# A gated cross-attention and expert layer on one core: another order of the opening, inputs laid out by the host, and the first block's routing moved

## The reference, cut to what matters

```python
x = x + tanh(g_xattn) * (softmax(q k^T / 4) v  W_o^T + b_o)   # q from layernorm(x), k and v from the context, 16 heads of 16
z = layernorm(x); h = layernorm(z) * ln_g + ln_b              # second half
logits = h @ Wr; top 2 of 7 experts, softmax of the two values as gates
# each expert takes at most 732 tokens, counted in the order of first choices, then second choices
routed = sum over kept choices of gate * (silu(h @ W1) * (h @ W3)) @ W2
shared = (silu(h @ W1s) * (h @ W3s)) @ W2s
x = x + tanh(g_ffn) * (routed + shared)
```

## Time and profile before

| | us |
|---|---|
| median of 3 runs | 910.91 (910.74 to 912.74) |
| the profiled execution, its own time | 909.93 |
| its span, first to last instruction | 908.2 |
| PE busy | 826.7 (91%) |
| DVE busy | 609.4 (67%) |
| ACT busy | 385.8 (42%) |
| POOL busy | 326.0 (36%) |

### The profile page before, as it was taken

How to read it: one execution, slowest core, us unless ns; L and a number is a source line. 1 busy time by engine, 2 the same in 40 slices (tenths; PEclk the granted TensorE clock), 3 DMA queues, 4 the chain that set the end, 5 groups by cost and what they waited for, 6 DMA issues and landing times.

```text
span 908.2 us, 14547 instructions
## 1 busy us (share of the span) xinstructions
PE 826.7 (91%) x5130; PEld 713.9 (79%) x5130; DVE 609.4 (67%) x1360; ACT 385.8 (42%) x718; POOL 326.0 (36%) x259
## 2 busy tenths in 40 slices
PE   4766799998999999999899999999999999999991
PEld 3533686885866858758687789999999999999991
DVE  5566877878779778787777766566665656565340
ACT  3254235336344254263535345354444545453330
POOL 5171403104013031040112840846547281823333
PEclk9868799999999999999999999999999999999996
DMA  6542041122400423203113332334434333431111
GB/s 170 139 140 63 10 117 36 44 74 49 117 15 21 116 49 69 56 27 93 36 43 119 110 99 93 83 87 103 85 102 82 86 74 104 97 66 19 16 19 19
DMA packets 97297, 66.93 MB, mean 74 GB/s; under 512 B 57910, under 2 KB 84716, under 8 KB 97240
## 3 DMA queue, kind: packets, MB, share of 16 engines
q1 hardware_dynamic: 43624, 55.40, 21.8%
q0 software_dynamic: 53088, 10.30, 8.3%
q10 hardware_dynamic: 528, 0.52, 0.2%
HBM read 37.38 MB, written 14.27 MB: 57 GB/s over the span
## 4 chain that ended last, share of the span: by engine, by line
PE 68%; DVE 13%; issue 7%; POOL 2%; ACT 1%; DVEq 0%; DMA 0%; POOLq 0%
PE bank L1367 19%; PE bank L1369 18%; PE bank L1368 18%; PE bank L1583 2%; PE bank L1584 2%; PE bank L1585 2%; DVE hidden L1097 2%; PE bank L1448 1%; PE bank L1621 1%; DVE bn_parts L1049 1%; DVE normed_heads L1101 1%; DVE row_max L1087 1%; DVE float_data L1170 1%; PE bank L1549 1%; DVE float_data L1068 1%
## 5 line engine op out<-in xcount | busy, mean ns | idle before, releaser
L1367 PE MATMUL bank<-split_operands 128*128 128x366 f32 (+4 forms) x1148 | 385.7, 336 | 15.2 <-DVE split_operands L1017 9.7
L1368 PE MATMUL bank<-split_operands 128*128 128x366 f32 (+4 forms) x1148 | 379.4, 331 | 0.0
L1369 PE MATMUL bank<-split_operands 128*128 128x366 f32 (+4 forms) x1148 | 379.3, 330 | 0.0
L1367 PEld LDWEIGHTS bank<-split_operands 128*128 128x128 f32 (+1 forms) x1148 | 217.2, 189 | 36.9 <-DVE split_operands L1022 7.2
L1369 PEld LDWEIGHTS bank<-split_operands 128*128 128x128 f32 (+1 forms) x1148 | 216.5, 189 | 12.4
L1368 PEld LDWEIGHTS bank<-split_operands 128*128 128x128 f32 (+1 forms) x1148 | 217.5, 189 | 9.7
L836 POOL DMA_INDIRECT out<-float_data,scatter_now x42 | 125.5, 2987 | 179.6 <-issue 93.0
L1350 DVE TENSOR_TENSOR hidden<-bank,float_data 128x366 f32<-128x366 f32 x112 | 60.4, 540 | 113.9 <-PE bank L1369 113.9
L1003 ACT ACTIVATE float_data<-bank 128x366 f32<-128x366 f32 x112 | 53.5, 477 | 113.7 <-PE bank L1369 113.7
L1000 ACT CAST split_operands<-hidden 128x366 fp32r<-128x366 f32 x112 | 55.7, 497 | 68.4 <-DVE hidden L1350 67.3
L812 POOL DMA_INDIRECT float_data<-z_scratch,gather_now x42 | 72.1, 1718 | 14.9 <-issue 14.0
(11 more groups left out here) (152 smaller groups left out, 1099.9 us busy)
## 6 DMA issues: line engine op xcount, KB each, us to landing
float_data<-in_L_ffn_W SPq DMA_DIRECT2D x21, 1024.0 KB, 8.6
split_operands<-split_operands SPq DMA_DIRECT2D x96, 128.0 KB, 2.3
float_data<-in_x SPq DMA_DIRECT2D x8, 512.0 KB, 4.8
z_scratch<-float_data SPq DMA_DIRECT2D x8, 512.0 KB, 3.1
out<-float_data SPq DMA_DIRECT2D x7, 512.0 KB, 2.8
split_operands<-split_operands SPq DMA_DIRECT2D x8, 192.0 KB, 3.8
float_data<-in_L_ffn_W1s SPq DMA_DIRECT2D x2, 512.0 KB, 4.1
float_data<-in_L_ffn_W3s SPq DMA_DIRECT2D x2, 512.0 KB, 4.9
```

The lines of the kernel that those rows point to most:

```text
L1367: pe.matmul(o, lhs[0], rhs[0], start=first, stop=False)
L1368: pe.matmul(o, lhs[0], rhs[1], start=False, stop=False)
L1369: return pe.matmul(o, lhs[1], rhs[0], start=False, stop=last)
```

## The change

1. **Inputs.** The host lays out the context (`ctx`), the four attention weights (`att`, with the rows of W_o already permuted) and all small inputs (`small`: biases, gains, gates, router) by partition. SP's first DMAs are twelve in place of 35 (three shared halves among them in both): the 16 loads of W_o and most of the small ones are gone.
2. **Opening.** The old steps are cut finer (`norm` into `stats_x`, `scale_x`, `residual`; queries and projection into the product and its reading out) and put in another order, below. W_v and W_o's low parts go from DVE to POOL. The four maxima of block 0 come before `project_values`; norm, transposes and queries of block 1 come after them, the queries between the halves of block 0's scores.
3. **Keys.** `kbd` is filled as soon as the high keys are there (`first_keys`), before the keys' scratch is written.
4. **Shared weights.** Halves 0 to 2 are loaded and cast beside block 0's maxima, 3 to 5 after block 0's projection; the low parts are made on POOL in three groups (6, 2 and 4 pieces), the second of them ahead of `norm2(0)`'s inverse root on POOL's queue.
5. **`norm2(0)`** stands between the third and the fourth maxima of block 1. With it, SP's store of z and load of x come before `stack_maxima(1)`.
6. **Block 0's routing.** `transpose_z(0)`, `logits(0)`, `logits_T(0)`, `choose(0)`, `count(0)`, `counted(0)`, `slots(0)` and `place(0)` and the norm of block 2 move from the end of `first_period` and the start of period 1 into the later part of period 1.
7. **Banks.** Block 0 and 1 use two PSUM banks (4, 5) in turn for the value products, with a new semaphore `pv_read` for when DVE has read one; the other banks are dealt out anew.

```diff
 def first_period(do, b):
     n = b.next()
+    do("context")
+    do("weights", 1)
     do("project_keys")
-    do("norm", b)
-    do("keys_lo")
+    do("stats_x", b)
+    do("weights", 0)
+    do("scale_x", b)
+    do("bias_keys")
     do("transpose_x", b)
-    do("norm", n)
+    do("weights", 2)
     do("queries", b)
+    do("queries_out", b)
+    do("keys", b)
+    do("residual", b)
+    do("stack", b)
+    do("shared_weights", 0)
+    for t in range(TT):
+        do("maxima", b, t)
     do("project_values")
-    do("keys", b)
-    do("stack", b)
-    do("maxima", b, 0)
-    do("maxima", b, 1)
-    do("transpose_x", n)
-    do("maxima", b, 2)
-    do("maxima", b, 3)
     do("maxima_T", b)
     do("stack_maxima", b)
+    do("values_out")
+    norm(do, n)
+    do("first_scores", b)
+    do("transpose_x", n)
     do("route_const")
+    do("scores", b, 0)
     do("queries", n)
-    do("first_scores", b)
-    for half in range(2):
-        do("scores", b, half)
+    do("scores", b, 1)
+    do("queries_out", n)
     do("stack", n)
+    do("attention_hi", b)
     do("maxima", n, 0)
     do("maxima", n, 1)
-    do("attention_hi", b)
     do("project", b)
+    do("project_out", b)
+    do("shared_weights", 1)
     do("maxima", n, 2)
+    do("norm2", b)
     do("maxima", n, 3)
     do("maxima_T", n)
     do("stack_maxima", n)
-    do("norm2", b)
-    do("transpose_z", b)
+    do("shared_rest")
     do("first_scores", n)
-    do("logits", b)
-    do("logits_T", b)
-    do("choose", b)
-    do("norm", n.next())
...
     do("scores", b, 0)
     if b.at(1):
-        do("count", f)
-        do("counted", f)
-        do("slots", f)
+        do("transpose_z", f)
     do("scores", b, 1)
+    if b.at(1):
+        nxt("stats_x")
     up(0)
-    do("place", f)
+    if b.at(1):
+        nxt("scale_x")
+        nxt("residual")
+    else:
+        do("place", f)
     do("attention_hi", b)
+    if b.at(1):
+        do("logits", f)
     up(1)
+    if b.at(1):
+        do("logits_T", f)
     nxt("transpose_x")
     up(2)
     do("project", b)
+    do("project_out", b)
     nxt("queries")
+    nxt("queries_out")
     nxt("stack")
     do("norm2", b)
+    if b.at(1):
+        do("choose", f)
     down(0)
     down(1)
     nxt("maxima", 0)
     up(3)
-    do("transpose_z", b)
-    up(4)
+    if b.at(1):
+        do("count", f)
+        do("counted", f)
+        do("slots", f)
+        up(4)
+        do("place", f)
+        do("transpose_z", b)
+    else:
+        do("transpose_z", b)
+        up(4)
     down(2)
     do("logits", b)
...
+def pv_bank(b, p):
+    return 4 + (p // 2 % 2 if b.at(0) or b.at(1) else p // 2)
...
         def transpose_x(b):
...
+            if b.at(2):
+                pe.wait_ge(sig["lg_done"], 1)
...
         def maxima(b, t):
             if b.at(0):
                 if t == 0:
-                    pe.wait_ge(sig["v_ready"], B)
...
         def logits(b):
...
+            if b.at(1):
+                pe.wait_ge(sig["place_added"], 1)
...
         def count(b):
             pe.wait_ge(sig["r_onehots"], b.n + 1)
+            if b.at(0):
+                pe.wait_ge(sig["m_done"], 2 * TT + 1)
...
-            if p == 4:
-                if b.at(1):
-                    pe.wait_ge(sig["hl_ready"], KD)
...
-            if p == 6 and b.at(1):
-                pe.wait_ge(sig["counts_read"], 1)
+            if b.at(0) or b.at(1):
+                if p >= 4:
+                    pe.wait_ge(sig["pv_read"], b.n * 4 + p // 2 - 1)
```

More of the change, by code:

```diff
@@ L189, in period @@
     if not b.at(NB - 2):
-        do("norm", n.next())
+        norm(do, n.next())
     down(7)
@@ L542, in _ @@
         sp.sem_inc(out_stored[1], 16)
[L543 to L555, removed]
@@ new lines, in load_shared, with first_keys @@
+        def load_shared(h):
+            if h >= 3:
+                sp.wait_ge(sig["wsplit_lo"], NSTEP0 + 2 * (h - 2))
+            if h == 5:
+                sp.wait_ge(sig["xT_ready"], 2 * KD)
+            m, part = h // 2, h % 2
+            kk = wsv[m].shape[1] // 2
+            sp.dma_start(sh_stage[h].rearrange("p (k f) -> p k f", k=kk), wsv[m][:, part * kk:(part + 1) * kk])\
+              .then_inc(shared_loaded[h % 3], 16)
+        for h in range(3):
+            load_shared(h)
+        def first_keys():
+            sp.wait_ge(sig["zeros_ready"], 1)
+            sp.wait_ge(sig["k_hi"], KD)
+            for j in range(8):
+                sp.dma_start(kbd[16 * j:16 * j + 16, :, j, :].bitcast(F32), k_s[16 * j:16 * j + 16, 0, :, 0:SK].bitcast(F32))\
+                  .then_inc(sig["kbd_loaded"], 16)
@@ L586, in project_keys, with more_shared @@
                 sp.dma_start(kscr[j].rearrange("(k p) t -> p k t", p=P), k_s[:, j].bitcast(F32)).then_inc(sig["k_stored"], 16)
[L588 to L595, removed]
-        for h in range(3):
-            load_shared(h)
-        def load_more_shared(b, half):
-            if b.at(0) and half == 0:
+        def more_shared(half):
+            if half == 1:
                 for h in range(3, 6):
@@ L608, in load_keys @@
                 bt = b.i
[L609 to L615, removed]
+                if not b.at(0):
+                    sp.wait_ge(sig["m_done"], b.n * TT)
+                    kd = kscr.rearrange("s (g j d) (b t) -> s j d g b t", g=KD, j=8, b=B)
+                    for j in range(8):
+                        sp.dma_start(kbd[16 * j:16 * j + 16, :, j, :].bitcast(F32), kd[0, j, :, :, bt, :])\
+                          .then_inc(sig["kbd_loaded"], 16)
                 sp.wait_ge(sig["k_stored"], 32)
@@ L819, in first_gather @@
             gather(Turn(0, 1))
-        token_blocks(pool, {"norm": norm, "scores": attention_lo, "stack": stationary_values, "norm2": norm2,
+        token_blocks(pool, {"stats_x": stats_x, "residual": residual, "weights": weights, "shared_weights": shared_weights,
+                            "shared_rest": shared_rest, "values_out": first_values, "scores": attention_lo, "stack": stationary_values, "norm2": norm2,
                             "route_const": route_const, "first_pieces": split_pieces, "slots": onehot_values,
@@ L1299, in last_pieces @@
                                   W1_[:, 0, m, cols].bitcast(F32), ALU.subtract).then_inc(sig["wsplit_lo"], 1)
-        token_blocks(dve, {"project_keys": project_keys, "keys_lo": keys_lo, "project_values": project_values, "norm": norm, "scores": scores, "transpose_x": transpose_x, "project": project,
-                           "queries": queries, "norm2": norm2, "transpose_z": transpose_z, "logits_T": logits_T,
+        token_blocks(dve, {"context": context, "weights": weights, "bias_keys": bias_keys, "values_out": values_out,
+                           "stats_x": stats_x, "scale_x": scale_x, "scores": scores, "transpose_x": transpose_x,
+                           "project_out": project_out, "queries_out": queries_out, "norm2": norm2, "transpose_z": transpose_z, "logits_T": logits_T,
                            "maxima": maxima, "up": up, "last_hidden": last_hidden, "shared_out": shared_out,
```

326 lines of the change are left out of this document (181 added, 145 removed).

## The result

The kernel after takes 926.18 us (median of 4 runs, 923.78 to 926.47), beside 911.60 us for the kernel before on the same chip. The ratio is 1.0155, with a 95% interval of 1.0142 to 1.0167: slower by some 14.6 us. The profiled execution took 926.31 us at a span of 924.1 us, 15.9 more than the span before. The prediction had the direction, but its 914.7 us and its range, 906 to 920, are too low.

The account below looks back on a forecast made before the run. The prediction took PE, busy 91% of the span, as the bound. Its terms, 6.5 - 1.9 - 9.4 = -4.8 us, made the profiled 909.93 us into 914.7, with a range of 906 to 920.

Parts of the forecast that it names:

- the large give-back: Period 1, first down to block 1's logits: 9.4 us lost, as block 0's routing delays place(0).
- Step 1: Opening, up to block 1's first scores: at 75.7 instead of 77.95 us, 2.2 us earlier.
- Scaling 1.4: norm2(0)'s scaling on VectorE, ahead of block 1's fourth reduction, was taken to last 1.4 us.
- the 0.8 us for SP's two transfers: Delay of block 1's stacked maxima by z's store and x's load just ahead: 0.8 us, between bounds 0 and 5.6.
- Step 2: Block 1's scores up to up(0,0): at 91.0 instead of 97.56 us, 6.5 us earlier.
- Rival 3: Clock falls in period 1, at the gap ahead of place(0) and once more, 2 us each: 918 us; chance 0.14.
- Step 3: Period 1, first down to block 1's logits: 20.7 us instead of 11.3, so 9.4 us given back.

Follow-up runs that it names:

- e1: The kernel after, with GpSimd's last four low parts of the shared weights made to wait until norm2(0)'s scaling is done: 922.46 us, ratio 1.0113.
- e10: e1 with GpSimd's pieces 6 and 7 also moved behind norm2(0)'s inverse root: 920.00 us, ratio 1.0086.
- e3: The kernel after, with 58 extra unused matmuls in TensorE's gap, around the transposes of block 1's maxima: 922.00 us, ratio 1.0115.
- e8: e2 with choose(0) right behind logits_T(0), and count, counted and slots ahead of the first down: 915.95 us, ratio 1.0028.
- e2: The kernel after, with only norm2(0) moved back behind stack_maxima(1): 919.12 us, ratio 1.0057.
- e4: e2 with block 0's routing and block 2's norm put back where the kernel before has them: 911.66 us, ratio 0.9985.
- e6: e4 with e1's wait and 28 extra unused matmuls in TensorE's gap ahead of block 1's scores: 907.22 us, ratio 0.9946.
- e9: e8 with the 58 extra matmuls of e3: 918.31 us, ratio 1.0063.

## Why the prediction was wrong in size

**What held.** All of the difference is made ahead of block 1's logits, and the large give-back is the one that was named. From the first `down` to `place(0)` the prediction had 15.3 us and the trace has 15.45; the idle time there was to be some 4 us and is 4.23, released by GpSimd's one-hot values; ahead of `count` 1.2 and 1.40. From `up(0,0)` to the first `down` 1.9 us were to be given back, and 1.4 were. Block 0's first scores came 1.7 us earlier than predicted. Some sums of the walk are 0.1 to 0.4 us above their own terms (GpSimd free at 34.8, where 23.8 + 2.8 + 7.8 is 34.4); none of this makes the miss.

**Step 1 that failed: "To block 1's first scores: only 2.2 us earlier".** They came 3.8 later, a miss of 6.0 us. Two terms of the step were wrong. "Scaling 1.4" ran beside GpSimd's pieces and took 5.16, which is 3.8 of the miss (e1: 3.5 us at this mark, 3.7 in time). And the load that was to be issued at 60.1, with GpSimd's two pieces done at 66.6, was issued at 62.40, and they ended at 69.6: 3 us more (e10 gives 2.0 at the mark, since VectorE's third reduction ends only at 69.2 there). Against this stands the 0.8 us for SP's two transfers, which do not show: from the issue of the stacked maxima at 79.37 it is 2.35 us to the first score, as before.

The load was late in the main because block 0's scores were long. Timelines: VectorE's low parts of block 1's queries after, then the load's issue in e3.

```profile
56.42 1.37 DVE L1147 SCALAR_TENSOR_TENSOR split_operands<-bank,small_inputs,split_operands 128x512 fp32r<-128x512 f32 x2
...
59.57 0.59 SPq L621 DMA_DIRECT2D float_data<-in_L_ffn_W3s  x1
```

From block 0's first scores to these low parts the walk has 21.0 us (35.1 to 56.1), and the trace 24.4 (33.41 to 57.79), with the clock at 0.50 in the midst of it. In e3, where the clock rose early, the load is issued at 59.57.

I carried over 1.4 us from a row with a free GpSimd without bounding it. The trace of before could have warned me. Timeline of DVE before: one kind of operation beside GpSimd's pieces of 45.91 to 61.46, and with GpSimd idle.

```profile
47.27 1.44 DVE L1101 TENSOR_TENSOR normed_heads<-hidden,recip_den 128x256 f32<-128x256 f32 x1
...
163.92 0.42 DVE L1101 TENSOR_TENSOR normed_heads<-hidden,recip_den 128x256 f32<-128x256 f32 x1
```

For a scaling there was no such row, but there was one for its engine. The Trainium skill, SBUF — State Buffer, "SBUF: two separate sides", says that VectorE and GpSimd share a pair of SBUF ports, and that the pair is an exclusive lock, held for a whole instruction, between a GpSimd operation and a VectorE operation in a two-port mode or with two SBUF inputs. An estimate by this section of the Trainium skill, if the scalings run in such a mode and each waits for one piece of 1.27 us, is 4 x 1.27 = 5.1 us. The trace agrees with 5.16; the mode and the port it does not show.

**Step 2: "To up(0,0): 6.5 us earlier".** The walk had 15.3 us from the first scores; it was 19.4. It priced exponentials and waits at the rows' durations and took no fall of the clock in this stage. The wait of 5.12 us is gone as predicted, but with the clock at 0.50 TensorE is busy for 17.16 us of the stage, and it is as long as before. e3 shows the size: 14.4 us at 0.92. Rival 3 had this kind of cost, but priced it in period 1 and at 2 us a time; of the opening it said only that it has such gaps.

**Step 3, mis-sized: "Downs to logits(1): 9.4 us given back".** It was 11.0. The order and the waits are as predicted up to `place(0)`. Behind it the clock was low: `place` took 1.88 us (0.97 in e8) and the transposes of z 1.93 (1.03 in the earlier trace rows), and the `down` behind them began at the low clock too. This is rival 3 in the place that it named, worth 1.6 us.

The sum: 6.0 for step 1, 4.1 for step 2, 1.6 for step 3, less 0.5 for the stretch to the downs, is 11.2. Added to the predicted 4.8 it is 16.0, and the spans differ by 15.9.

**The move of `norm2(0)`** by itself costs 7.1 us (e2), and e2 is still 0.6% slower than the kernel before. The rest is the routing's place: e4 brings 7.5 us of it back.

## What to carry to other kernels

A step on a second engine's queue has to be read twice: for what waits behind it, and for what runs beside it. Before costing a VectorE operation from SBUF at its usual duration, look at what GpSimd does in those microseconds; a single wait on GpSimd was worth 3.7 us here. And where a chain of small steps stands decides what it costs: block 0's routing made block 1's scores 1.4 us longer (20.8 in e4, 19.4 in e2), and the stretch to block 1's logits, where TensorE has no time to spare, 12 us longer (41.7 against 29.6). Last, read an experiment's trace ahead of the stage that it is about: the profiled executions of e3 and e9 were some 3 us ahead before their first extra matmul ran.

## What the runs showed of the hardware that I had not expected

- Four VectorE `tensor_scalar` of 128x256 from SBUF to SBUF took 5.16 us beside GpSimd's 128x512 `tensor_tensor` (5.17 in e2) and 1.38 alone. VectorE's reduction of 128x462 from PSUM beside the same GpSimd operation, at 67.14, took 1.54 us for three of them, its usual time.
- After 4.66 us without TensorE work (e2), and after waits of 1.83 and 0.76 us with little work between them (e6), the granted clock was 0.50 for the next 24 and 16 us, though TensorE was busy for most of that time. In the kernel before it was back at 1.00 by 84 us, 6 us into block 1's scores, though TensorE was busy for only 13.15 of their 19.61 us. Why it rises in the one and not in the other is open.
- In block 0's scores the clock rose to 1.00 by 42 us in two traces (e3, e9) and only near 49 us in the other traces of the new opening. Block 1's last maxima came some 3 us sooner with it.
- A store and a load of 512 KB each, issued some 3 us ahead of two small copies within SBUF, did not delay them: 2.35 us from issue to use, as without them.
